# Graph attention over 100,000 edges: no memsets between the gathers, eight part gathers behind the last

## Chip, cores, metric

One core of a Trainium2 chip runs the kernel. The metric is the device time of one execution in microseconds; smaller is better.

## What is computed

6250 nodes with 96 features, 100,000 edges (src, dst) sorted by dst, and 96 features for each edge. With 8 heads of 12:

```python
Q, K, V = (x @ Wq + bq), (x @ Wk + bk), (x @ Wv + bv)       # per node
E = edge_attr @ We + be                                       # per edge
score = exp(clip(sum_head(K[src] * Q[dst] / sqrt(12) * E), -5, 5))
wV = segment_sum(V[src] * score, dst);  Z = segment_sum(score, dst)
out = layernorm(x + wV / (Z + 1e-6))
```

All in float32. The rows of K and V that the edges name in no order (`src`) have to be gathered; `dst` is sorted, so 512 edges in a row touch a window of fewer than 80 nodes.

## The kernel before

A first stage makes a table in device memory, `kv_table`, with a row of 192 values (K and V, 768 bytes) for each node, and `q_table` for Q. The edges are then worked off in 196 groups of 512 (`GROUPS`, `GROUP`), each of four tiles of 128 edges (the last group has two tiles, the very last tile 32 edges). All engines run the same sequence of groups, each at its own lag, held together by semaphores.

What each engine does for a group, in the variant `windowed(True)` that these inputs take:

- **GpSimd (POOL)** fetches the K and V rows of the four tiles with one indirect DMA each (`gather`, L490 to 495): one row of `kv_table` for each of 128 partitions, into one of 16 ring slots of `kv`. The first 8 groups (`EARLY`) gather rows of x instead, 32 gathers of 384 bytes a row, from which K and V are made on the core. Behind each gather stands a call of `space` (L497): a memset of 128 x 128 values of a buffer that nothing reads, with a wait for the memset before it.
- **TensorE** (L1015 to 1087) makes in its iteration i the product of the edge features of group i with We (L1023), the product that picks the query rows of group i (L1030), transposes the product of both of group i-2 (`turn`, L1041), and sums by node for group i-5 (`segment_sums`, L1055).
- **ScalarE** makes the one-hot matrix for the query product (L588, L591), copies the features' product out of PSUM (L597) and takes exponentials (L602, L603).
- **VectorE** (L870 to 896) multiplies queries and features of group i (L751), multiplies the gathered K rows of group i-2 with them (`times_keys`, L761; it waits for the group's four gathers and its turn), makes the one-hot matrix for the sums (L743), adds by head (L768), weighs the gathered V rows (L782) and adds a finished group's sums to the accumulator (L797).
- **SyncE (SP)** loads edge features, relative node numbers and query windows eight groups ahead (L414, L418, L422), and stores finished rows (L439).

Order of the gathers. Groups 8 to 15 go without a gate, 16 to 31 wait for the ring slot (`e_msg`: the group 16 before has been weighed). From group 32 on (`PACED_FROM`) each of the four gathers waits for a signal of TensorE, L518:

```python
pool.wait_ge(*((e_seg, group - 3), (e_e, ahead + 1), (e_q, ahead + 1), (e_turn, group + 1))[t])
```

with `ahead = group + 2`: the first for the sums of group-4, the second and third for the features' and the queries' product of group+2, the fourth for the turn of the group itself. In TensorE's order these are four steps in a row, from iteration group+1 to group+2.

Node rows that no later edge touches are divided, normalised and stored along the way; after the last group a short drain does the rest on VectorE and ScalarE, and SP stores it.

Of the kernel before, what the change touches and what calls it, by code (L numbers as in the profile page):

```python
# [31 lines left out]
F32 = mybir.dt.float32  # L32
# [7 lines left out]
P = 128  # L40
# [6 lines left out]
GROUP_TILES = 4  # L47
GROUP = GROUP_TILES * P
GROUPS = -(-N_EDGES // GROUP)
# [27 lines left out]
FIRST_TILES = [*range(0, NODE_TILES - LAST_TILES, FINAL_TILES), NODE_TILES - LAST_TILES, NODE_TILES]  # L77
STEPS = len(FIRST_TILES) - 1
FINAL_RING = 3
KV_RING, EA_RING, REL_RING, QWIN_RING, PICK_RING, MSG_RING = 16, 8, 8, 8, 4, 4  # L80
QE_RING = 3

# [12 lines left out]
def tiles_of(group):  # L95
    return min(GROUP_TILES, TILES - group * GROUP_TILES)


def edges_in(tile):
    return min(P, N_EDGES - tile * P)  # L100
# [25 lines left out]
def stores_of(step):  # L126

    first, n = FIRST_TILES[step], tiles_in(step)
    whole = min(n, N_NODES // P - first)
    return [(0, whole, P)] * (whole > 0) + [(whole, 1, N_NODES % P)] * (whole < n)  # L130


def stores_before(step):

    return sum(len(stores_of(s)) for s in range(step % FINAL_RING, step, FINAL_RING))


def build(nc, xT, x_rows, src_cols, dst_cols, dst_rows, eaT, weights, biases, ones, out):
# [16 lines left out]
    kv_table = nc.dram_tensor("kv_table", [TABLE_ROWS, 2 * DIM], F32).ap()  # L155
# [5 lines left out]
    with ExitStack() as ctx:  # L161
        def sb(name, shape, dt):
            return ctx.enter_context(nc.sbuf_tensor(name, shape, dt))
# [4 lines left out]
        def sem(name):  # L168
            return ctx.enter_context(nc.semaphore(name))
# [21 lines left out]
        stage_row = node_stage[:].rearrange("p t d -> p (t d)")  # L191
        result_cols, msg_cols = 2 * FINAL_RING * FINAL_TILES * DIM, MSG_RING * GROUP_TILES * SUMS
        results = stage_row[:, 0:result_cols].rearrange(
            "p (b s t d) -> p b s t d", b=2, s=FINAL_RING, t=FINAL_TILES)
        msg = stage_row[:, result_cols:][:, 0:msg_cols].rearrange(
# [6 lines left out]
        src_idx = sb("src_idx", [P, GROUPS * GROUP_TILES], U32)  # L202
# [21 lines left out]
        kv = sb("kv", [P, KV_RING, GROUP_TILES, 2 * DIM], F32)  # L224
# [11 lines left out]
        rows_f = acc_t[0:PAIRS, 0:2 * GROUP].rearrange("p (j e) -> p j e", j=2)  # L236


        spacer = sb("spacer", [P, 128], F32)
        g_src = sb("g_src", [P, GROUP_TILES], U32)  # L240
        g_dst = sb("g_dst", [P, GROUP_TILES], U32)
        g_dst_f = sb("g_dst_f", [P, GROUP_TILES], F32)
# [5 lines left out]

        z_inv = sb("z_inv", [P, FINAL_RING, FINAL_TILES, HEADS], F32)
        z_eps = sb("z_eps", [P, FINAL_RING, FINAL_TILES, HEADS], F32)  # L250
        stats = sb("stats", [P, FINAL_RING, FINAL_TILES, 6], F32)
        moments = sb("moments", [P, FINAL_RING, FINAL_TILES, 2], F32)
# [64 lines left out]
        e_msg = sem("e_msg")  # L317
        e_seg = sem("e_seg")
        e_acc = sem("e_acc")
        e_space = sem("e_space")  # L320
        g_free = sem("g_free")
        g_idx = sem("g_idx")
        g_step = sem("g_step")
# [31 lines left out]
        def path_of(eng):  # L355
            eng.wait_ge(r_ready, 1)
            return eng.value_load(path_i[0:1, 0:1], min_val=GENERAL, max_val=STREAMED)
# [6 lines left out]
        def all_tables_stored(eng):  # L364
            for i in range(UNITS_IN_RING):

                eng.wait_ge(d_table[i], 32 * len(range(i, UNITS, UNITS_IN_RING)))

        def by_path(eng, path, windowed, general):

            with eng.If(path == STREAMED):
                windowed(True)
            with eng.Else():
                with eng.If(path == WINDOWED):
                    windowed(False)
                with eng.Else():
                    general()
# [103 lines left out]
        @block.gpsimd  # L481
        def _(pool):
            nc.gpsimd.memset(ident[:], 0.0).then_inc(c_id0, 1)
            pool.wait_ge(c_id0, 1)
            nc.gpsimd.affine_select(out=ident[:], in_=ident[:], compare_op=ALU.not_equal, fill=1.0, base=0,
                                    pattern=[[-1, P]], channel_multiplier=1).then_inc(c_ident, 1)
            nc.gpsimd.iota(iota_i[:], pattern=[[1, SPAN]], base=0, channel_multiplier=0).then_inc(c_iota, 1)
            nc.gpsimd.iota(part_i[:], pattern=[[1, 1]], base=0, channel_multiplier=1).then_inc(c_iota, 1)

            def gather(rows, table, group, t, semaphore):  # L490
                tile = group * GROUP_TILES + t
                n = edges_in(tile)
                pool.indirect_dma_start(rows[0:n, :], None, table,  # L493
                                        bass.IndirectOffsetOnAxis(ap=src_idx[0:n, tile:tile + 1], axis=0)
                                        ).then_inc(semaphore, 16)

            def space(tile):  # L497
                if tile:
                    pool.wait_ge(e_space, tile)
                nc.gpsimd.memset(spacer[:], 0.0).then_inc(e_space, 1)  # L500

            pool.wait_ge(l_src_early, 16)
            for group in range(EARLY):
                for t in range(GROUP_TILES):
                    gather(kv[:, group, t, 0:DIM], x_rows, group, t, e_kv[group])
                    space(group * GROUP_TILES + t)
            pool.wait_ge(l_src, 16)
            all_tables_stored(pool)
            path = path_of(pool)

            def windowed(streamed):
                for group in range(EARLY, GROUPS):
                    slot, ahead = group % KV_RING, min(group + 2, GROUPS - 1)
                    if KV_RING <= group < PACED_FROM:
                        pool.wait_ge(e_msg, group - KV_RING + 1)
                    for t in range(tiles_of(group)):
                        if group >= PACED_FROM:
                            pool.wait_ge(*((e_seg, group - 3), (e_e, ahead + 1), (e_q, ahead + 1), (e_turn, group + 1))[t])  # L518
                        gather(kv[:, slot, t, :], kv_table, group, t, e_kv[slot])
                        space(group * GROUP_TILES + t)  # L520

            def general():
                pool.wait_ge(l_dst, 16)
                pool.wait_ge(x_kv, 2 * EARLY)
                with pool.Fori(0, GROUPS) as group:
                    pool.wait_ge(g_free, group + 1)
                    cols = bass.ds(group * GROUP_TILES, GROUP_TILES)
                    nc.gpsimd.tensor_copy(g_src[:], src_idx[:, cols]).then_inc(g_idx, 1)
                    nc.gpsimd.tensor_copy(g_dst[:], dst_idx[:, cols]).then_inc(g_idx, 1)
                    pool.wait_ge(g_idx, group * 2 + 2)  # L530
                    pool.sem_inc(g_step, 1)
                    for t in range(GROUP_TILES):
                        pool.indirect_dma_start(
                            kv[:, 0, t, :], None, kv_table,
                            bass.IndirectOffsetOnAxis(ap=g_src[:, t:t + 1], axis=0)).then_inc(g_gather, 16)
                        pool.indirect_dma_start(
                            g_q[:, t, :], None, q_table,
                            bass.IndirectOffsetOnAxis(ap=g_dst[:, t:t + 1], axis=0)).then_inc(g_gather, 16)

            by_path(pool, path, windowed, general)  # L540


# [605 lines left out]
```

## Time and profile before

| | |
|---|---|
| median of 3 timed runs | 1074.79 us (1072.62 to 1075.31) |
| span of the profiled execution, first to last instruction | 1231.7 us |
| busy in it: GpSimd, TensorE, VectorE, ScalarE | 919.8, 824.3, 595.7, 457.8 us |
| mean granted clock of TensorE | 0.81 of full speed |
| DMA: moved, mean rate | 153.29 MB, 124 GB/s |

The durations below come from the one profiled execution, whose own time is known by its span of 1231.7 us; the timed runs are executions without a profile. Busy time doesn't count semaphore waits or the issuing of plain DMAs. A gather is an instruction of POOL in the profile (DMA_INDIRECT), and its time is the time on POOL, not that until the data have landed. "remote" and "issue" in a row say that the idle time ahead of an instruction ended with an event that the profile can't name, or with none that it shows.

### The profile page before, as it was taken

The numbers are of one execution on the slowest core, as the hardware profiler recorded it, in microseconds if no ns is written. First come the engines' busy times: TensorE is split into PE (matmuls) and PEld (weight loads), VectorE is DVE, ScalarE is ACT, GpSimd is POOL, SyncE is SP. The second block draws the span as 40 slices with busy tenths as digits, with TensorE's granted clock in tenths as the row PEclk, the third lists the DMA queues.
The fourth block names the chain that finished last, engine by engine and source line by source line (L and its number), as shares of the span: only waits on it lengthen the run. The fifth ranks groups of instructions, "written<-read, shape, count | busy, mean of one in ns | idle before, by whom it ended". The sixth has DMA issues, their size and how long they took to land.

```text
span 1231.7 us, 13818 instructions
## 1 busy us (share of the span) xinstructions
PE 824.3 (67%) x3375; PEld 455.9 (37%) x3375; DVE 595.7 (48%) x1583; ACT 457.8 (37%) x1094; POOL 919.8 (75%) x1572
## 2 busy tenths in 40 slices
PE   6518565986676666667676667666767676776763
PEld 4415232543343333333333334333333333333433
DVE  5104344954444464445444545445554545454645
ACT  3206232743343343333333334333434343433331
POOL 8882777167878778778787787887777877877783
PEclk9757787988877888887888787887878877878885
DMA  9922344454545445445444444444444444444321
GB/s 245 277 77 77 104 126 109 137 145 120 144 116 138 125 112 131 125 111 127 122 121 125 108 135 117 120 132 120 111 130 125 128 127 112 121 130 126 92 77 51
DMA packets 124525, 153.29 MB, mean 124 GB/s; under 512 B 57885, under 2 KB 92191, under 8 KB 124436
## 3 DMA queue, kind: packets, MB, share of 16 engines
q0 software_dynamic: 37008, 75.28, 23.9%
q1 hardware_dynamic: 80608, 73.74, 21.7%
q10 hardware_dynamic: 6822, 3.31, 1.0%
q8 instruction: 31, 0.51, 0.2%
q14 instruction: 56, 0.46, 0.1%
HBM read 142.26 MB, written 9.98 MB: 124 GB/s over the span
## 4 chain that ended last, share of the span: by engine, by line
POOL 37%; PE 22%; issue 16%; another core or an unknown queue 10%; DVE 6%; DMA 6%; ACT 2%; SPq 0%; DVEq 0%; POOLq 0%
POOL kv L493 30%; POOL spacer L500 7%; DMA kv<-kv_table,src_idx 5%; PE ps_eq L1030 4%; PE ps_eq L1023 4%; PE ps_qe_seg L1055 3%; PE ps_last L1055 3%; PE ps_eq_qe L1023 2%; PE ps_qe_seg L1041 2%; PE ps_eq_qe L1030 1%; PE ps_eq_qe L1041 1%; DVE ps_last L768 1%; DVE node_stage L743 1%; DMA w_all<-biases_in 1%
## 5 line engine op out<-in xcount | busy, mean ns | idle before, releaser
L493 POOL DMA_INDIRECT kv<-kv_table,src_idx x750 | 714.2, 952 | 285.5 <-issue 114.7
L602 ACT ACTIVATE ps_last<-clipped 128x32 f32<-128x32 f32 x196 | 39.4, 201 | 542.4 <-issue 397.2
L1030 PE MATMUL ps_eq<-pick_t,q_win 128*96 128x512 f32 (+1 forms) x262 | 169.5, 735 | 78.7 <-ACT e_t L597 58.4
L761 DVE TENSOR_TENSOR kq<-kv,ps_qe_seg 128x384 f32<-128x384 f32 x98 | 53.9, 550 | 260.7 <-DMA kv<-kv_table,src_idx 195.7
L1023 PE MATMUL ps_eq<-ea,w_all 128*96 128x512 f32 (+1 forms) x262 | 172.5, 747 | 8.1 <-issue 7.4
L500 POOL MEMSET spacer<- 128x128 f32 x782 | 172.8, 221 | 2.7 <-remote 2.2
L761 DVE TENSOR_TENSOR kq<-kv,ps_eq_qe 128x384 f32<-128x384 f32 x98 | 54.1, 552 | 238.3 <-DMA kv<-kv_table,src_idx 175.5
L1055 PE MATMUL ps_qe_seg<-node_stage 128*104 128x80 f32 x784 | 116.2, 306 | 54.5 <-issue 28.9
L1055 PE MATMUL ps_last<-node_stage 128*104 128x80 f32 x780 | 108.2, 292 | 49.3 <-issue 24.2
L588 ACT ACTIVATE distance<-rel_bc,neg_part 80x512 bf16<-80x512 bf16 x196 | 138.4, 706 | 1.8 <-issue 0.6
L1055 PEld LDWEIGHTS ps_qe_seg<-node_stage 128*104 128x104 f32 x784 | 105.2, 218 | 64.6 <-issue 49.6
L591 ACT ACTIVATE pick_t<-distance 80x512 f32<-80x512 bf16 x196 | 123.2, 629 | 6.2
L1055 PEld LDWEIGHTS ps_last<-node_stage 128*104 128x104 f32 x780 | 97.7, 205 | 58.0 <-issue 33.5
L1030 PEld LDWEIGHTS ps_eq<-pick_t,q_win 128*96 128x96 f32 x262 | 46.4, 199 | 195.0 <-issue 194.4
L597 ACT COPY e_t<-ps_eq 96x512 f32<-96x512 f32 x131 | 74.3, 567 | 92.6 <-remote 58.2
L768 DVE TENSOR_REDUCE ps_last<-kq 128x32 f32<-128x384 f32 x196 | 107.6, 549 | 0.1
L782 DVE TENSOR_TENSOR node_stage<-kv,ps_last 128x384 f32<-128x384 f32 x196 | 106.3, 542 | 0.0
L1041 PE MATMUL ps_qe_seg<-ident,qe_t 96*128 96x96 f32 x390 | 60.0, 285 | 65.9 <-issue 41.2
L1030 PE MATMUL ps_eq_qe<-pick_t,q_win 128*96 128x512 f32 x130 | 82.6, 722 | 31.7 <-issue 15.8
L1041 PEld LDWEIGHTS ps_qe_seg<-ident,qe_t 96*128 96x128 f32 x390 | 48.3, 164 | 146.1 <-issue 103.4
L751 DVE TENSOR_TENSOR qe_t<-e_t,ps_eq 96x512 f32<-96x512 f32 x131 | 88.3, 674 | 17.5 <-PE ps_eq L1030 8.9
L1041 PEld LDWEIGHTS ps_eq_qe<-ident,qe_t 96*128 96x128 f32 x392 | 48.3, 160 | 125.9 <-issue 92.3
(90 smaller groups left out, 788.2 us busy)
## 6 DMA issues: line engine op xcount, KB each, us to landing
ea<-ea_t_in SPq DMA_DIRECT2D x196, 192.0 KB
rel_bc<-rel_rows_dram SPq DMA_DIRECT2D x196, 80.0 KB
kv<-kv_table,src_idx POOLq DMA_INDIRECT x750
q_win<-q_table SPq DMA_DIRECT2D x196, 30.0 KB
kv_table<-node_stage SPq DMA_DIRECT2D x5, 576.0 KB
x_both<-x_t_in SPq DMA_DIRECT2D x5, 480.0 KB, 8.9
x_both<-x_rows_in ACTq DMA_DIRECT2D x10, 240.0 KB
out<-node_stage SPq DMA_DIRECT2D x11, 192.0 KB
```

The lines of the kernel that those rows point to most:

```text
L493: pool.indirect_dma_start(rows[0:n, :], None, table, bass.IndirectOffsetOnAxis(ap=src_idx[0:n, tile:tile + 1], axis=0)).then_inc(semaphore ...
L500: nc.gpsimd.memset(spacer[:], 0.0).then_inc(e_space, 1)
L588: nc.scalar.activation(distance[:, b, 0:n], rel_bc[:, slot, 0:n], ACT.Abs, bias=neg_part[0:WINDOW, :]).then_inc(e_dist, 1)
L591: nc.scalar.activation(pick_t[0:WINDOW, group % 3, 0:n], distance[:, b, 0:n], ACT.Relu, bias=1.0, scale=-1.0).then_inc(e_pt, 1)
L751: nc.vector.tensor_tensor(qe_t[:, group % QE_RING, 0:n], e_t[:, group % 2, 0:n], ps_eq[(2 * group + 1) % 3][0:DIM, 0:n], ALU.mult).then_in ...
L761: nc.vector.tensor_tensor(kq[:, group % 2, 0:n, :], kv[:, slot, 0:n, 0:DIM], ps_qe[group % 2][:, 0:n * DIM].rearrange("p (t d) -> p t d", ...
L768: nc.vector.tensor_reduce(score[:, group % 2, 0:n, :], kq[:, group % 2, 0:n, :].rearrange("p t (h d) -> p t h d", h=HEADS), axis=AX_X, op= ...
L782: nc.vector.tensor_tensor(m[:, :, 0:DIM].rearrange("p t (h d) -> p t h d", h=HEADS), kv[:, group % KV_RING, 0:n, DIM:2 * DIM].rearrange("p ...
L1023: nc.tensor.matmul(ps_eq[2 * group % 3][0:DIM, 0:n], w_e, ea[:, slot, 0:n], start=True, stop=True).then_inc(e_e, 1)
L1030: nc.tensor.matmul(ps_eq[(2 * group + 1) % 3][0:DIM, 0:n], q_win[:, slot, :], pick_t[:, group % 3, 0:n], start=True, stop=True).then_inc(e ...
L1041: last = nc.tensor.transpose(ps_qe[group % 2][:, t * DIM:(t + 1) * DIM], qe_t[:, group % QE_RING, t * P:(t + 1) * P], ident[0:DIM, 0:DIM])
L1055: last = nc.tensor.matmul(ps_seg[group % 2][0:SUMS, 0:WINDOW], msg[:, group % MSG_RING, t, :], pick[:, group % PICK_RING, t, :], start=(t ...
```

## The change

The buffer `spacer`, its semaphore and the function `space` go, so that gathers follow each other on POOL with nothing but their own waits between them. The waits at L515 and L518 stay. Behind the last gather of group 195 POOL waits until group 180 has been weighed, issues eight more gathers of 127, 125, 121, 120, 112, 64, 16 and 2 rows of `kv_table` into slots 4 and 5 of the ring, which nothing reads any more, and waits for them.

```diff
+PARTS = (127, 125, 121, 120, 112, 64, 16, 2)
...
-        spacer = sb("spacer", [P, 128], F32)
...
-        e_space = sem("e_space")
+        e_part = sem("e_part")
...
-            def space(tile):
-                if tile:
-                    pool.wait_ge(e_space, tile)
-                nc.gpsimd.memset(spacer[:], 0.0).then_inc(e_space, 1)
-
             pool.wait_ge(l_src_early, 16)
             for group in range(EARLY):
                 for t in range(GROUP_TILES):
                     gather(kv[:, group, t, 0:DIM], x_rows, group, t, e_kv[group])
-                    space(group * GROUP_TILES + t)
...
                         gather(kv[:, slot, t, :], kv_table, group, t, e_kv[slot])
-                        space(group * GROUP_TILES + t)
+                part_gathers()
+
+            def part_gathers():
+
+                slot = GROUPS % KV_RING
+                pool.wait_ge(e_msg, GROUPS - KV_RING + 1)
+                for i, n in enumerate(PARTS):
+                    pool.indirect_dma_start(kv[0:n, slot + i // GROUP_TILES, i % GROUP_TILES, :], None, kv_table,
+                                            bass.IndirectOffsetOnAxis(ap=src_idx[0:n, i:i + 1], axis=0)
+                                            ).then_inc(e_part, 16)
+                pool.wait_ge(e_part, 16 * len(PARTS))
```

## Rows read from the trace of the kernel before

**Rows 1.** The page: span, and busy time of each engine with its share and instructions

```profile
span 1231.7 us, 13818 instructions
...
PE 824.3 (67%) x3375; PEld 455.9 (37%) x3375; DVE 595.7 (48%) x1583; ACT 457.8 (37%) x1094; POOL 919.8 (75%) x1572
```

**Rows 2.** The page: the chain that ended last, by line, shares of the span

```profile
POOL kv L493 30%; POOL spacer L500 7%; DMA kv<-kv_table,src_idx 5%; PE ps_eq L1030 4%; PE ps_eq L1023 4%; PE ps_qe_seg L1055 3%; PE ps_last L1055 3%; PE ps_eq_qe L1023 2%; PE ps_qe_seg L1041 2%; PE ps_eq_qe L1030 1%; PE ps_eq_qe L1041 1%; DVE ps_last L768 1%; DVE node_stage L743 1%; DMA w_all<-biases_in 1%
```

**Rows 3.** The page's groups of instructions: busy us, mean ns, idle before

```profile
L493 POOL DMA_INDIRECT kv<-kv_table,src_idx x750 | 714.2, 952 | 285.5 <-issue 114.7
...
L500 POOL MEMSET spacer<- 128x128 f32 x782 | 172.8, 221 | 2.7 <-remote 2.2
```

**Rows 4.** Instructions of L493, the first 32 gathers: ns min/median/max, first and last start

```profile
L493 POOL DMA_INDIRECT kv<-x_rows_in,src_idx x32: 950/950/2569, 4.6 to 49.0; - x32
```

**Rows 5.** The waits of all engines: us in total, times, longest

```profile
DVE kq L761 <- DMA kv<-kv_table,src_idx: 371.2, 131, 5.4
```

**Rows 6.** POOL's timeline: start us, us, what

```profile
255.28 0.95 POOL L493 DMA_INDIRECT kv<-kv_table,src_idx  x1 [0.17 <-issue]
256.23 0.22 POOL L500 MEMSET spacer<- 128x128 f32 x1
256.62 0.95 POOL L493 DMA_INDIRECT kv<-kv_table,src_idx  x1 [0.17 <-issue]
```

**Rows 7.** L761 by stretches: its busy time (x instructions), clock, DMA share, GB/s

```profile
119.00:219.00 100.00, 9.03 (x17) 0.78 0.43 118
219.00:254.00 35.00, 7.35 (x14) 1.00 0.49 133
254.00:1215.00 961.00, 90.25 (x163) 0.81 0.46 121
```

**Rows 8.** L493 in the paced stretch, the same columns

```profile
254.00:1215.00 961.00, 621.88 (x653) 0.81 0.46 121
```

**Rows 9.** All engines while POOL pauses: busy us of PE, PEld, DVE, ACT, POOL

```profile
219.00:254.00 35.00, 33.50 (x193) 20.34 (x193) 34.93 (x93) 27.26 (x65) 0.06 (x1) 1.00 0.49 133
```

**Rows 10.** POOL's timeline, group 32's first gather

```profile
253.94 0.95 POOL L493 DMA_INDIRECT kv<-kv_table,src_idx  x1 [34.98 <-PE ps_qe_seg L1055]
```

**Rows 11.** POOL's timeline, two gathers behind a stop

```profile
460.00 0.95 POOL L493 DMA_INDIRECT kv<-kv_table,src_idx  x1 [1.92 <-remote]
...
477.71 0.95 POOL L493 DMA_INDIRECT kv<-kv_table,src_idx  x1 [1.84 <-remote]
```

**Rows 12.** Timeline of all engines, 278 to 288 us

```profile
278.89 0.49 PE L1041 MATMUL ps_qe_seg<-ident,qe_t 96*128 96x96 f32 x4
...
283.41 0.56 DVE L761 TENSOR_TENSOR kq<-kv,ps_eq_qe 128x384 f32<-128x384 f32 x1 [2.53 <-DMA kv<-kv_table,src_idx]
...
284.75 0.55 DVE L782 TENSOR_TENSOR node_stage<-kv,ps_last 128x384 f32<-128x384 f32 x1
...
287.75 0.58 ACT L597 COPY e_t<-ps_eq_qe 96x512 f32<-96x512 f32 x1 [0.46 <-PE ps_eq L1023]
...
287.85 0.95 POOL L493 DMA_INDIRECT kv<-kv_table,src_idx  x1 [1.77 <-remote]
```

**Rows 13.** Timeline of all engines in the unpaced stretch, 193 to 206 us

```profile
193.86 1.94 PE L1023 MATMUL ps_eq<-ea,w_all 128*96 128x512 f32 x2
...
202.01 0.95 POOL L493 DMA_INDIRECT kv<-kv_table,src_idx  x1 [0.17 <-issue]
...
205.09 0.58 ACT L597 COPY e_t<-ps_eq 96x512 f32<-96x512 f32 x1 [13.64 <-remote]
```

**Rows 14.** Timeline of the end

```profile
1215.28 0.88 POOL L493 DMA_INDIRECT kv<-kv_table,src_idx  x1 [0.17 <-issue]
...
1217.01 9.79 SPq L439 DMA_DIRECT2D out<-node_stage  x4
1217.58 0.35 DVE L761 TENSOR_TENSOR kq<-kv,ps_qe_seg 128x192 f32<-128x192 f32 x1 [0.97 <-DMA kv<-kv_table,src_idx]
```

**Rows 15.** DMA queues of the page: packets, MB, share of 16 engines

```profile
q0 software_dynamic: 37008, 75.28, 23.9%
```

## Prediction

> **What bounds the kernel now.** I read the page's head, its chain and its groups first. GpSimd (POOL) is busy for 919.8 of 1231.7 us, TensorE for 824.3 and VectorE for 595.7 [rows 1]; the chain that ended last gives 30% to the gathers of L493 and 7% to the spacers of L500 [rows 2]. The groups are 782 gathers of 0.95 us and 782 memsets of 0.22 us [rows 3, 4], and the waits show VectorE's product with the gathered keys (L761) idle for 371.2 us until gathers land [rows 5]. Then POOL's timeline: the memset starts where the gather ends, the next gather 0.17 us behind the memset, and gathers start 1.34 us apart [rows 6]. Four make 5.34 us for a group of 512 edges.
>
> Is that the group's period? Between 254 and 1215 us VectorE makes 163 groups' products in 961 us, 5.90 us each, over 653 gathers, 1.472 us each [rows 7, 8]. So 1.336 of 1.472 us is POOL's own step and 0.136 us (89 us in all) is waiting. What the others could do shows where POOL pauses: from 219 to 254 us they live on sixteen groups gathered ahead and do 14 in 35 us, 2.5 us each, with TensorE at clock 1.00 (2.4 GHz) and busy for 33.50 us, 2.4 us a group [rows 7, 9]. They need less than half of the period; POOL sets it.
>
> The 89 us come as holds: POOL stops some 1.6 us about every 17.7 us, as before 460.00 and 477.71 [rows 11]. One from near by: the gather at 287.85 is the fourth of group 37 (counted from 253.94 [rows 10], group 32's first), and its gate, the turn of group 37, is by the same counting the one of 278.89, done 8.5 us before. ScalarE's copy, which waits for a TensorE signal too, starts at 287.75 [rows 12]. Signals of TensorE seem to reach the others late while gathers run, and at once when POOL stops. The unpaced stretch shows it stronger: a product over the features ends at 195.80, and ScalarE takes it at 205.09 after 13.64 us of idling, 2 us after the last gather of a run ended at 202.96 [rows 13].
>
> **Profile and timed runs.** The span is 1231.7 us, the median 1074.79: the profiled execution is 157 us longer. POOL's instructions alone give 782 x 1.336 = 1045 us, with 4.6 us before the first gather and 15.5 us from the end of the last to the end 1065 us [rows 4, 6, 14], 10 us under the median. If the steps last as long there, timed runs hardly wait and are POOL's chain from end to end; the holds and most of the slow start would belong to the profiled execution. I subtract POOL's saving from both, and keep the holds for the rivals.
>
> **The change, part by part.**
>
> *Spacers go.* 782 memsets of 0.22 us [rows 3], and with each a wait for the memset before, long satisfied. What then stands between two gathers, no row shows. Bounds: the gap of 0.17 us goes too, a step is 0.95 us and 0.386 us are saved; or it stays, the step is 1.12 us and 0.216 us are saved [rows 6]. A gain below 0.216 would need longer gathers, a loss gathers over 1.34 us; the nearest row for that is the longest of the first 32, 2.57 us, once, beside the loads of the start [rows 4]. I take the gap to stay: every gather has it ahead, no memset has. In the paced stretch that is 653 x 0.216 = 141 us (bound 252). The first 128 gathers could give 28 us (bound 49), but the others need 34 iterations of 2.5 us before group 32's gather may go, and in the profile they come so late that POOL idles for 34.98 us [rows 10]. I count half, 14 us.
>
> The Trainium skill, GPSIMD Engine Reference, section "Instruction dispatch", warns that a core of GpSimd starts the next instruction as soon as it has done its own share of the last. By that rule the gap needn't stand between two gathers, and the sum would be that of the first rival below. The memsets, which follow gathers without a gap, agree with it; the 0.17 us ahead of every gather does not.
>
> *The gates stay.* From group 32 on each gather waits for a TensorE signal, and a faster POOL meets them closer. The round: a fourth gather lands 1.4 us after its end (1216.16 to 1217.58) [rows 14], product to weighing take 1.9 us (283.41 to 285.30) [rows 12], TensorE's sums, features, queries and turn 2.4 us, the gather 1.12 us: 7 us. The turn of group g follows the sums of g-4, weighed behind the keys of g-3, so that is for three groups, 2.3 us each: no bound. With a signal 8.5 us late it is 15.5 us, 5.2 us each, and would bind; that is for the rivals. At TensorE's lower level (1.2 GHz) its 2.4 us become 4.8, over POOL's 4 x 1.12 = 4.48. The mean clock of 0.81 puts 38% of the stretch at that level [rows 7]: 0.3 us x 0.38 x 163 = 19 us at most; I take 10 us back, since less idling should keep the clock up more often.
>
> *DMA.* Gathers come up to 19% faster; the queues' share in the stretch goes from 0.46 [rows 7] to 0.55 at most. Nothing.
>
> *Eight gathers at the end.* Issued from 1216.2 on: 8 x 1.12 = 9 us, landing 1.4 us later, POOL is done near 1226.7. VectorE's drain and the last stores (four issued between 1217.01 and 1226.80, the end at 1231.7) [rows 14] hide it with 5 us to spare; without that cover it would cost all of 10 us. Their gate is satisfied long before, and 687 rows of 768 bytes are 0.53 MB. Bounds: 0 and 10 us; I take 0.
>
> The Trainium skill, DMA: Bandwidth & Descriptors, section "Why a DMA increments its semaphore by 16 and not by 1", has a DMA use the largest number of engines, up to 16, that divides its partitions: one for 127, five for 125, eleven for 121, fifteen for 120. No row shows such a gather. The queue's row, 23.9% of sixteen engines for 75.28 MB [rows 15], gives 63 us of one engine per MB, so an estimate by this rule is 6 us on one engine for 127 rows; if the last stores queued behind it the sum would be 6 us more, 936.
>
> **Sum.** 1074.8 - 141 - 14 + 10 = 930 us. For the profiled span 1231.7 - 141 + 10 = 1101, since POOL doesn't set the start there.
>
> **The rivals.**
>
> *The gap goes too.* Step 0.95 us: 1074.8 - 252 - 14 = 809, and with all of the start 774, less what the lower clock takes (a group of 3.8 us against 4.8): about 800. For it: memsets need no gap. 0.12.
>
> *Holds take part of it.* POOL meets late signals sooner: 0.6 holds of 1.6 us per group against 0.33 now, 4.48 + 0.96 = 5.44 against 5.90 us, 75 us saved: 1000 us. For it: the late signals of [rows 12]. Against: a gate not met stops POOL, and the stop lets all signals through. 0.15.
>
> *Slower: gathers without a spacer hold TensorE's signals up.* Place: POOL's gates in the paced stretch. If the 0.39 us between gathers is what lets signals pass, each group needs a stop: 4.48 + 1.6 = 6.08 us against 5.90, 163 x 0.18 = 30 us, 1105; if timed runs had no holds before, 0.74 x 163 = 120 us, 1195. It decides from 0.89 holds per group. For it: the unpaced stretch, 17 groups in 100 us although their keys lay ready [rows 7], and the 13.64 us [rows 13]. Against: a median that leaves 10 us for all holds. 0.21.
>
> *No change.* The round with late signals sets the period (5.2 us above, with landings of 2 us 5.4), and what POOL saves becomes waiting at its gates: 1072 to 1078. Against: 1.336 us steps fill the median already. 0.05.
>
> **How the numbers follow.** The forecast has 0.47 (its own range 890 to 960), the others as above. About 0.3% is what a measurement of this kernel can tell from no change: faster by more 0.74, within 0.05, slower 0.21. The range goes from 800, the bound without a gap, to 1105, the slower case at its nearer price; its farther half and a little below 800 are left out.
>
> **What would show it.** No memsets of L500; gathers starting 1.12 us apart (0.95 for the first rival); about 4.6 us per group between group 32 and the end, plus holds; L761's idle time before landings down from 371 us by some 140; no more than 0.4 holds per group; eight more gathers behind the last, none in the chain. Wrong if gathers lengthen back to back (over 1.3 us each nothing is left), if stops of 1.6 us come in nearly every group, or if POOL's end takes the place of the last stores.

## The result, and the profile after

The changed kernel takes 1014.51 us (1013.26 to 1015.47, 4 runs) where the kernel before takes 1074.63 us (1072.62 to 1075.31, 4 runs): a ratio of 0.9444, with a 95% interval of 0.943 to 0.9457, so 60 us faster. The forecast was 930 us and 145 us faster. The direction was right, the size was not. In every run here the timed figure is 1.8 to 2.0 us longer than the span of the same execution (1014.0 against 1012.2).

The page of the changed kernel, head, a queue's row, chain by line and the gathers' group, against [rows 1, 15, 2, 3]:

```profile
span 1012.2 us, 13044 instructions
...
PE 757.0 (75%) x3375; PEld 417.5 (41%) x3375; DVE 594.2 (59%) x1583; ACT 452.7 (45%) x1094; POOL 751.9 (74%) x798
...
q0 software_dynamic: 37712, 75.81, 28.7%
...
POOL kv L493 35%; DMA kv<-kv_table,src_idx 16%; PE ps_eq L1034 3%; PE ps_eq L1027 3%; PE ps_last L1059 2%; DVE node_stage L747 2%; DVE ps_last L772 2%; PE ps_eq_qe L1027 2%; PE ps_eq_qe L1034 2%; PE ps_qe_seg L1059 1%; DVE kq L765 1%; PE ps_qe_seg L1045 1%; PE ps_eq_qe L1045 1%; DMA q_table<-node_stage 1%; POOL kv L521 1%
...
L493 POOL DMA_INDIRECT kv<-kv_table,src_idx x750 | 709.6, 946 | 233.8 <-issue 196.6
```

The 172.8 us of memsets are gone, the gathers last as long as before (946 against 952 ns), and the chain is still that of the gathers and of their landings. But their idle time ahead, 233.8 us for 750, is 0.31 us each. GpSimd's timeline shows it, against [rows 6]:

```profile
399.23 0.95 POOL L493 DMA_INDIRECT kv<-kv_table,src_idx  x1 [0.30 <-issue]
...
400.49 0.95 POOL L493 DMA_INDIRECT kv<-kv_table,src_idx  x1 [0.31 <-PE ps_eq_qe L1045]
...
401.74 0.95 POOL L493 DMA_INDIRECT kv<-kv_table,src_idx  x1 [0.30 <-issue]
```

Gathers start 1.25 us apart, not 1.12: between two gathers stand 0.30 us, where 0.17 stood between a memset and a gather. The second row names TensorE as what ended the 0.31 us, but the gap is the same where nothing was waited for; a releaser beside a gap of the plain size is no hold.

The longest waits, against [rows 5], and the time of L765 (VectorE's product with the keys, L761 before) by stretches, against [rows 7]:

```profile
DVE kq L765 <- DMA kv<-kv_table,src_idx: 361.7, 162, 5.1
POOL kv L493 <- issue: 205.7, 658, 5.5
```

```profile
119.00:219.00 100.00, 11.33 (x21) 0.90 0.60 161
219.00:254.00 35.00, 4.18 (x8) 0.95 0.57 155
254.00:988.00 734.00, 80.78 (x146) 0.86 0.52 140
```

VectorE still waits 361.7 us for landings. No stop of 1.6 us as in [rows 11] is left, and no pause of 35 us as in [rows 10]: from 254 us on a group takes 734/146 = 5.03 us, and 4 x 1.25 is 5.00. Behind 254 us no gap ahead of a gather is over 0.5 us: the gates (the waits of L518) hold no gather here.

The end, against [rows 14]: GpSimd's and VectorE's last instructions.

```profile
988.57 0.88 POOL L493 DMA_INDIRECT kv<-kv_table,src_idx  x1 [0.30 <-issue]
989.75 2.55 POOL L521 DMA_INDIRECT kv<-kv_table,src_idx  x1 [0.30 <-issue]
992.60 1.20 POOL L521 DMA_INDIRECT kv<-kv_table,src_idx  x1 [0.30 <-issue]
994.11 1.02 POOL L521 DMA_INDIRECT kv<-kv_table,src_idx  x1 [0.30 <-issue]
995.43 0.97 POOL L521 DMA_INDIRECT kv<-kv_table,src_idx  x1 [0.30 <-issue]
996.71 0.96 POOL L521 DMA_INDIRECT kv<-kv_table,src_idx  x1 [0.31 <-issue]
997.97 0.91 POOL L521 DMA_INDIRECT kv<-kv_table,src_idx  x1 [0.30 <-issue]
999.18 0.86 POOL L521 DMA_INDIRECT kv<-kv_table,src_idx  x1 [0.30 <-issue]
...
999.64 0.81 DVE L862 TENSOR_SCALAR node_stage<-node_stage,moments,rstd 128x96 f32<-128x96 f32 x3 [0.67 <-ACT rstd L617]
1000.35 0.88 POOL L521 DMA_INDIRECT kv<-kv_table,src_idx  x1 [0.30 <-issue]
```

The eight part gathers (called the eight below; 127, 125, 121, 120, 112, 64, 16 and 2 rows, in that order) take 11.8 us with their gaps, the first alone 2.55. GpSimd is done at 1001.23, behind VectorE's last instruction (1000.45), and the span ends 11.8 us behind VectorE, where before it ended 5.7 us behind it (1225.98 to 1231.7). What is still moving in the last 7.7 us of the changed kernel, by the DMA queues between 1004.5 and 1012.2 us:

```profile
q14 instruction: 4, 0.03, 1.3%
```

That is the only queue with packets there: the gathered rows and the stored ones have landed by then.

### The profile page after: what moved, and what is told of

The parts are those of the page before. It is cut to its first block, busy times and chain, and to the rows that moved or that the text cites. A ratio compares the mean times of both kernels' runs of the same rounds, so it can differ in the third digit from the quotient of the medians.

```text
span 1012.2 us, 13044 instructions
## 1 busy us (share of the span) xinstructions
PE 757.0 (75%) x3375; PEld 417.5 (41%) x3375; DVE 594.2 (59%) x1583; ACT 452.7 (45%) x1094; POOL 751.9 (74%) x798
## 4 chain that ended last, share of the span: by engine, by line
POOL 36%; PE 19%; DMA 18%; issue 15%; DVE 7%; ACT 3%; SPq 0%; DVEq 0%; ACTq 0%
POOL kv L493 35%; DMA kv<-kv_table,src_idx 16%; PE ps_eq L1034 3%; PE ps_eq L1027 3%; PE ps_last L1059 2%; DVE node_stage L747 2%; DVE ps_last L772 2%; PE ps_eq_qe L1027 2%; PE ps_eq_qe L1034 2%; PE ps_qe_seg L1059 1%; DVE kq L765 1%; PE ps_qe_seg L1045 1%; PE ps_eq_qe L1045 1%; DMA q_table<-node_stage 1%; POOL kv L521 1%
## 5 line engine op out<-in xcount | busy, mean ns | idle before, releaser
L493 POOL DMA_INDIRECT kv<-kv_table,src_idx x750 | 709.6, 946 | 233.8 <-issue 196.6
L1034 PE MATMUL ps_eq<-pick_t,q_win 128*96 128x512 f32 (+1 forms) x262 | 161.3, 702 | 19.5 <-ACT e_t L601 18.2
L1027 PE MATMUL ps_eq<-ea,w_all 128*96 128x512 f32 (+1 forms) x262 | 158.9, 692 | 7.3 <-DVE qe_t L755 5.8
L765 DVE TENSOR_TENSOR kq<-kv,ps_qe_seg 128x384 f32<-128x384 f32 x98 | 54.0, 551 | 187.8 <-DMA kv<-kv_table,src_idx 187.7
L765 DVE TENSOR_TENSOR kq<-kv,ps_eq_qe 128x384 f32<-128x384 f32 x98 | 54.1, 552 | 174.0 <-DMA kv<-kv_table,src_idx 174.0
L1059 PE MATMUL ps_qe_seg<-node_stage 128*104 128x80 f32 x784 | 101.7, 280 | 57.0 <-DVE acc_t L801 43.4
L1059 PE MATMUL ps_last<-node_stage 128*104 128x80 f32 x780 | 102.9, 282 | 54.9 <-DVE acc_t L801 45.9
L1059 PEld LDWEIGHTS ps_qe_seg<-node_stage 128*104 128x104 f32 x784 | 91.5, 193 | 65.4 <-DVE node_stage L786 50.4
L1059 PEld LDWEIGHTS ps_last<-node_stage 128*104 128x104 f32 x780 | 92.1, 195 | 63.9 <-DVE node_stage L786 53.8
L747 DVE TENSOR_TENSOR node_stage<-ps_last,rel_f 128x320 f32<-128x320 f32 x196 | 94.5, 482 | 0.5 <-ACT ps_last L606 0.5
L1027 PE MATMUL ps_eq_qe<-ea,w_all 128*96 128x512 f32 x130 | 84.4, 737 | 4.4 <-DVE qe_t L755 4.4
L1045 PE MATMUL ps_qe_seg<-ident,qe_t 96*128 96x96 f32 x390 | 54.7, 266 | 36.6 <-DVE kq L765 36.5
L1034 PE MATMUL ps_eq_qe<-pick_t,q_win 128*96 128x512 f32 x130 | 75.4, 665 | 6.3 <-ACT e_t L601 5.9
```

The source lines that it names most:

```text
L493: pool.indirect_dma_start(rows[0:n, :], None, table, bass.IndirectOffsetOnAxis(ap=src_idx[0:n, tile:tile + 1], axis=0)).then_inc(semaphore ...
L747: nc.vector.tensor_tensor(pick[:, group % PICK_RING, 0:n, :], window_iota.unsqueeze(1).to_broadcast([P, n, WINDOW]), rel.unsqueeze(2).to_b ...
L765: nc.vector.tensor_tensor(kq[:, group % 2, 0:n, :], kv[:, slot, 0:n, 0:DIM], ps_qe[group % 2][:, 0:n * DIM].rearrange("p (t d) -> p t d", ...
L1027: nc.tensor.matmul(ps_eq[2 * group % 3][0:DIM, 0:n], w_e, ea[:, slot, 0:n], start=True, stop=True).then_inc(e_e, 1)
L1034: nc.tensor.matmul(ps_eq[(2 * group + 1) % 3][0:DIM, 0:n], q_win[:, slot, :], pick_t[:, group % 3, 0:n], start=True, stop=True).then_inc(e ...
L1045: last = nc.tensor.transpose(ps_qe[group % 2][:, t * DIM:(t + 1) * DIM], qe_t[:, group % QE_RING, t * P:(t + 1) * P], ident[0:DIM, 0:DIM])
```

## The experiments

Chips are of two sorts for this kernel: on some the kernel before has a median of 1071 to 1075 us (the first sort below), on others of 1218 to 1232 us (the second), and no single run of it lay between (1070 to 1075 and 1214 to 1239 us). No chip was measured at two times, so whether this belongs to the chip or to a state that it was in isn't shown. Each kernel ran beside the kernel before on the same chip, and kernels with the same number in the second column shared a chip; across chips only ratios are compared. The result above is of the first sort; the trace that the prediction was read from, 1231.7 us long, looks like the second. Of the kernel before there is no trace on the first sort.

| kernel | before there, us | median, us | ratio, 95% interval |
|---|---|---|---|
| changed kernel, again | 1071.02 | 1012.17 | 0.9448 (0.9433 to 0.9464) |
| changed kernel, a third time | 1071.37 | 1012.97 | 0.9449 (0.9433 to 0.9464) |
| without the eight | 1073.66 | 1008.98 | 0.9399 (0.9384 to 0.9415) |
| without the eight and the gates, 1 | 1071.02 | 1006.70 | 0.9396 (0.938 to 0.9412) |
| without the eight and the gates, 2 | 1073.66 | 1008.84 | 0.9398 (0.9383 to 0.9414) |
| without the eight and the gates, 3 | 1071.37 | 1006.23 | 0.939 (0.9374 to 0.9406) |
| without the eight and the gates, with one-column spacer | 1073.66 | 1008.93 | 0.9395 (0.938 to 0.9411) |
| before, 256-column spacer | 1073.66 | 1157.70 | 1.0782 (1.0764 to 1.08) |
| without the eight | 1217.77 | 1230.17 | 1.0103 (1.0078 to 1.0128) |
| without the eight | 1231.42 | 1240.94 | 1.0084 (1.006 to 1.0108) |
| before, one-column spacer | 1217.77 | 1232.32 | 1.0134 (1.0104 to 1.0164) |
| before, one-column spacer | 1231.42 | 1247.31 | 1.014 (1.0111 to 1.0169) |
| before, one-column spacer with semaphore | 1217.77 | 1232.37 | 1.0127 (1.0103 to 1.0152) |
| before, with the eight | 1217.77 | 1220.12 | 1.0035 (1.0014 to 1.0056) |
| before, with the eight | 1231.42 | 1236.95 | 1.0054 (1.0029 to 1.008) |
| changed, other sizes of the eight | 1231.42 | 1250.53 | 1.0168 (1.0138 to 1.0197) |
| changed, other sizes of the eight | 1231.61 | 1252.49 | 1.016 (1.0101 to 1.0218) |
| without the eight and the gates, 4 | 1231.61 | 1337.93 | 1.0854 (1.0792 to 1.0916) |

**Is GpSimd's step (from the start of one gather to the start of the next) all that bounds?** The spacer made larger, in the kernel before:

```
-        spacer = sb("spacer", [P, 128], F32)
+        spacer = sb("spacer", [P, 256], F32)
```

> The kernel before with a spacer of 256 columns in place of 128. Theory A (GpSimd's step is the whole bound): each of the 782 steps longer by the memset's growth, which from 0.22 us for 128 columns is 0.05 to 0.13 us; 40 to 100 us slower than the kernel before where that takes 1071 us. Theory C (something else bounds too): less than half of the growth. Where the kernel before takes 1220 to 1230 us: GpSimd has idle time, so less than half of the growth is seen.

Its timeline on GpSimd, start and duration:

```profile
399.32 0.95 POOL L493 DMA_INDIRECT kv<-kv_table,src_idx  x1 [0.16 <-issue]
400.26 0.34 POOL L500 MEMSET spacer<- 128x256 f32 x1
400.76 0.95 POOL L493 DMA_INDIRECT kv<-kv_table,src_idx  x1 [0.16 <-issue]
```

A step of 1.45 us against the 1.34 of [rows 6]: 782 x 0.11 = 86 us, and 84.0 us were measured. That is theory A: on this sort of chip the time is 782 of GpSimd's steps and a start and an end around them, and a change to the step comes through whole.

**What is the gap of 0.30 us?** A memset of one column, without semaphore, in place of the spacer:

```
             def space(tile):
-                if tile:
-                    pool.wait_ge(e_space, tile)
-                nc.gpsimd.memset(spacer[:], 0.0).then_inc(e_space, 1)
+                nc.gpsimd.memset(spacer[:, tile:tile + 1], 0.0)
```

It ran three times: twice in the kernel before with its gates, and once added to the kernel without gates and without the eight.

> No waits on signals, no eight gathers, and a memset of one column after each gather. Where the kernel before takes 1071 us: Theory A (0.30 us is the gap between two DMA instructions, 0.17 us the one after a memset) a step of 1.22 us and 985 us, from 975 to 1000, with 1006.7 us without the memset; Theory B (0.30 us follows a gather in any case) 1071 us or more. Where the kernel before takes 1220 to 1230 us: near the kernel without waits and memset.

Its timeline on GpSimd:

```profile
399.95 0.95 POOL L494 DMA_INDIRECT kv<-kv_table,src_idx  x1 [0.19 <-issue]
400.90 0.11 POOL L499 MEMSET spacer<- 128x1 f32 x1
401.20 0.95 POOL L494 DMA_INDIRECT kv<-kv_table,src_idx  x1 [0.19 <-issue]
402.15 0.11 POOL L499 MEMSET spacer<- 128x1 f32 x1
```

Both theories miss: it takes 1008.93 us, and the kernel without it on the same chip 1008.84. The memset lies inside the 0.30 us: 0.95 + 0.11 + 0.19 is again 1.25. With 128 columns the sum is 0.95 + 0.22 + 0.17 = 1.34, with 256 it is 0.95 + 0.33 + 0.17 = 1.45 (0.34 and 0.16 in the rows shown). So some 0.30 us pass behind a gather before the next one, whether it is empty or a short memset fills it, and a memset adds only what it has beyond about 0.13 us. The step of 1.12 us that the forecast took was not to be had by taking the spacer out.

> The kernel before, with a spacer of one column in place of 128 and no semaphore on it. Theory A (the gap of 0.30 us is that between two DMA instructions on the queue of GpSimd, and one after a memset is 0.17): a step of 0.95 + memset of some 0.1 + 0.17 = 1.22 us, against 1.25 without a spacer; with the end as before about 985 us, from 975 to 1010. Theory B (0.30 us follows a gather whatever comes next, so a memset is only added to it): a step of 1.35 or more, 1075 us or above. Theory C (TensorE's signals start to hold the gathers up once the step is under some 1.25): no better than 1007 us, with idle time ahead of gathers put down to TensorE.

> As the spacer of one column, but with the semaphore set by it and waited for by the next. If the semaphore costs nothing on GpSimd: the same time as with no semaphore, within 3 us. If the signalling is a part of the spacer's price (a spacer took 0.22 us and the gap behind it 0.17): 0.02 to 0.06 us a step more, 15 to 50 us above the kernel without it.

> A spacer of one column and no semaphore, again, for a ground where the kernel before takes 1071 us. Theory A (0.30 us is the gap between two DMA instructions of GpSimd, 0.17 the one after a memset): a step of 0.95 + some 0.1 + 0.17 = 1.22 us; with the end as before about 985 us, from 975 to 1010. Theory B (0.30 us follows a gather whatever comes next): a step of 1.35 or more, 1071 us or above. Theory C (signals of TensorE hold gathers up once the step is under 1.25 us): no better than 1007 us. If the kernel before takes 1218 us again: 1232 us as in the first run.

These three fell on the second sort of chip, where nothing is to be gained by a shorter step (below): 1.0134, 1.0127 with the semaphore, and 1.014. The semaphore makes no difference within the intervals. The expected 975 to 1010 us can't be tested by the time there, but the step can: unhindered gathers start 1.25 us apart in all three traces, with a memset of 0.11 us and a gap of 0.19 us, where theory A had 1.22 and theory B 1.35.

**Do the gates hold gathers?** Without them (and without the eight) only the wait for a free slot stays:

```
-                    if KV_RING <= group < PACED_FROM:
+                    if KV_RING <= group:
                         pool.wait_ge(e_msg, group - KV_RING + 1)
                     for t in range(tiles_of(group)):
-                        if group >= PACED_FROM:
-                            pool.wait_ge(*((e_seg, group - 3), (e_e, ahead + 1), (e_q, ahead + 1), (e_turn, group + 1))[t])
...
-                part_gathers()
```

> The changed kernel without the eight gathers, and without the waits of the gathers on TensorE's and VectorE's signals; only the wait for a free slot stays, once a group. Where the kernel before takes 1075 us: no difference from a step of 1.25 us if the waits never hold a gather (1007 us within 3); if packed gathers delay others, slower. Where it takes 1218 us: Theory S1 (each signal that a gather waits for arrives late, and the waits are what makes it long): under 1100 us. Theory S2 (the gathers' own activity makes the signals late, and TensorE's chain is the bound): 1230 us or more.

> As before, the changed kernel without the waits on signals and without the eight gathers. Where the kernel before takes 1071 us: 1006.7 us again. Where it takes 1220 to 1230 us: Theory S1 (the gathers' waits on late signals make it long) under 1100 us; Theory S2 (TensorE's chain is the bound whatever GpSimd does) 1230 us or more.

> The changed kernel without the waits on signals and without the eight gathers, for the chips where the kernel before takes 1218 to 1231 us. Theory S1 (there the late signals hold the gathers, and the waits are what makes it long): the gathers run through at 1.25 us, under 1100 us. Theory S2 (TensorE's signals to VectorE and ScalarE are late too, and that chain is the bound): 1230 us or more, with the gathers held by the free slots. Where the kernel before takes 1071 to 1075 us: 0.94 of it, as twice.

0.9396, 0.9398 and 0.939 against 0.9399 with the gates; on the one chip that had both, 1008.84 against 1008.98 us. On the first sort of chip they cost and give nothing. The last of the three was meant for the second sort and fell on the first.

**What do the eight cost?**

```
                         gather(kv[:, slot, t, :], kv_table, group, t, e_kv[slot])
-                part_gathers()
```

> The changed kernel without the eight gathers, once more. Where the kernel before takes 1071 us: Theory A (the eight set the end) 1006 us, as without the waits (1006.7 us); Theory B (hidden) 1012 us. Where it takes 1220 to 1230 us: 1% slower than the kernel before, as twice.

> The changed kernel as it is, since the first four runs stood on a ground where the kernel before took 1217.8 us and not 1074.6. Where the kernel before takes 1075 us: 1014.5 us again. Where it takes 1218 us (TensorE's signals late, gathers held by their waits): Theory S (the late signals set that time, spacers or not): 1230 to 1240 us, no faster than before.

The changed kernel's ratio was 0.9448 and 0.9449; without the eight it is 0.9399: 0.005 of 1071 us, 5.3 us. The theory that the eight set the end holds; its 1006 us were for a chip at 1071 us, and this one was at 1073.66. Two chips had both the changed kernel and the one without the eight and the gates: there it is 5.5 us (1012.17 against 1006.70) and 6.7 us (1012.97 against 1006.23). The last instructions of the kernel without them, on GpSimd and VectorE:

```profile
989.55 0.88 POOL L493 DMA_INDIRECT kv<-kv_table,src_idx  x1 [0.30 <-issue]
...
1000.57 0.81 DVE L861 TENSOR_SCALAR node_stage<-node_stage,moments,rstd 128x96 f32<-128x96 f32 x3 [0.67 <-ACT rstd L616]
```

VectorE ends 10.95 us behind the last regular gather, as with the eight (11.00), and the span (1007.4) 6.0 us behind VectorE. With the eight it ends 11.0 us behind the last of them (1001.23 to 1012.2). So VectorE isn't slowed on this sort; the end waits for GpSimd's tail and for what comes behind it. Of the 11.0 us behind the last gather the landing of data is at most 3.3 (up to 1004.5 us, above); what the other 7.7 are isn't shown, nor whether the gathers or GpSimd's wait for them bring them in, since no run has the one without the other. This version, 1008.98 us, beats both kernels on the first sort.

Other sizes, 112 rows in place of the first four, were to tell whether the sizes or the number cost:

```
-PARTS = (127, 125, 121, 120, 112, 64, 16, 2)
+PARTS = (112, 112, 112, 112, 112, 64, 16, 2)
```

> The changed kernel with other sizes of the last eight gathers: 112 rows five times, 64, 16 and 2, in place of 127, 125, 121, 120, 112, 64, 16 and 2. Theory P1 (the end waits for as many instructions as there are, 1.2 us each; the one of 127 rows adds 1.6): 2 us under the changed kernel, 1010 us. Theory P2 (only gathers of odd sizes land late and hold the end): 6 to 7 us under, 1006 us. Theory P3 (hidden): 1012 us, the same.

> The changed kernel with 112 rows five times, 64, 16 and 2 as its last eight gathers. Where the kernel before takes 1071 to 1075 us: Theory P1 (the eight cost by the time that they take on GpSimd, behind which the end waits; the one of 127 rows takes 2.55 us and 112 rows 0.96): 2 us under the changed kernel, 0.943 of the kernel before. Theory P2 (only the odd sizes cost): 0.939 to 0.940, as without the eight. Theory P3 (sizes do not matter): 0.9448. Where it takes 1218 to 1231 us: 1.017 times, as in the first run.

It ran twice, both times on the second sort of chip, where its end is another one (VectorE 10.7 us behind GpSimd, 1245.11 against 1234.42 in the second run). Its timeline there, the last regular gather, the first and the last of the eight, and VectorE:

```profile
1223.80 0.88 POOL L493 DMA_INDIRECT kv<-kv_table,src_idx  x1 [0.31 <-issue]
1224.99 0.94 POOL L521 DMA_INDIRECT kv<-kv_table,src_idx  x1 [0.30 <-issue]
...
1233.54 0.88 POOL L521 DMA_INDIRECT kv<-kv_table,src_idx  x1 [0.30 <-issue]
1234.89 0.24 DVE L801 TENSOR_TENSOR acc_t<-acc_t,ps_qe_seg 104x80 f32 x1 [7.72 <-remote]
```

So 2.55 us is the price of 127 rows and not of the first place; 112 rows take 0.94 there. What each of the eight costs in time to the end on the first sort stays open. The last row shows what the eight do on the second sort: VectorE stands for 7.72 us while they run. TensorE's sums for it end at 1227.82; the trace's record of semaphores has their signal at 1234.77, 0.35 us behind the end of the last gather. VectorE ends 20.4 us behind the last regular gather there, and 10.9 in the kernel without the eight. The eight added to the kernel before:

> The kernel before with its spacers, and the eight gathers added after the last one. Theory A (they lie on the end): 7 us slower than the kernel before, about 1082 us. Theory B (hidden behind the weighing and the stores of the last group): 1075 us within 2.

> The kernel before with its spacers and the eight gathers added. Theory A (the eight set the end, by as much as in the changed kernel): 7 us slower than the kernel before, 1078 us. Theory B (hidden): 1071 us. If the kernel before takes 1218 us again: 1220 us as in the first run.

1.0035 and 1.0054 of the kernel before, 4 and 7 us by the ratios (2.4 and 5.5 by the medians), both intervals above 1: the eight aren't hidden there either, but theory A's 7 us are not settled by this. In the first of the two the span ends 22.50 us behind the last regular gather, in the kernel before 15.54.

**The other sort of chip.** The kernel without the eight is 1% slower than the kernel before there, where on the first sort it is 6% faster.

> The changed kernel without the eight gathers at the end. Theory A (the eight set the end: from the end of the last regular gather to the end of the span it is 22.8 us in the changed kernel and 15.5 us before): about 7 us less than the 1014.5 us of the changed kernel, so 1007 us. Theory B (the last stores set the end anyway, as the prediction had it): 1014 us within 2.

> The changed kernel without the eight gathers, again, for a ground where the kernel before takes 1071 us. Theory A (the eight set the end): 7 us under the changed kernel, 1005 to 1007 us, and the same as without the waits on signals (1006.7 us). Theory B (hidden): 1012 us. If the kernel before takes 1218 us again: 1230 us as in the first run.

Neither theory on the eight had 1230 or 1241 us; they were for the first sort. The second run was expected to be 1% slower here again, and is 0.8%. Waits of the second of these runs:

```profile
DVE kq L764 <- DMA kv<-kv_table,src_idx: 386.4, 129, 5.7
POOL kv L493 <- issue: 233.9, 673, 24.1
POOL kv L493 <- remote: 84.0, 53, 2.8
ACT e_t L600 <- remote: 81.4, 36, 16.3
```

and its group of gathers:

```profile
L493 POOL DMA_INDIRECT kv<-kv_table,src_idx x750 | 709.6, 946 | 465.6 <-issue 224.4 <-remote 84.0 <-PE ps_qe_seg L1058 49.2
```

Unhindered gathers are 1.25 us apart there too. Idle time beyond the gaps is 465.6 - 750 x 0.30 = 241 us, and was 285.5 - 750 x 0.17 = 158 us with the spacers [rows 3]: 83 us more of waiting. The steps save 750 x (0.22 - 0.13) = 68 us and the gathers 5; the sum is +10 us, and 9.5 were measured (the two profiled spans, from different chips, differ by 6.1). What the spacers' going saves comes back, and a little more, as stops at the gates. Then the gates were taken away there:

> The changed kernel without the waits on signals and without the eight gathers, tried again for a chip where the kernel before takes 1218 to 1231 us. Theory S1 (the gathers' waits on late signals make it long): under 1100 us. Theory S2 (TensorE's late signals to VectorE and ScalarE make it long): 1230 us or more. Where the kernel before takes 1071 to 1075 us: 0.939 of it again.

```profile
ACT e_t L598 <- remote: 523.1, 67, 16.1
...
POOL kv L493 <- DVE node_stage L783: 274.2, 53, 20.5
```

It is 106 us slower than the kernel before (1.0854), theory S2. ScalarE now waits 523.1 us, up to 16.1 us at a time, for signals whose sender had ended long before. One of them, from the timeline of all engines of that run (counted from the start, both rows are of group 80; ScalarE copies a product while TensorE is at the next):

```profile
604.33 1.04 PE L1024 MATMUL ps_eq<-ea,w_all 128*96 128x512 f32 x2
...
612.78 0.94 POOL L493 DMA_INDIRECT kv<-kv_table,src_idx  x1 [0.30 <-issue]
613.94 0.58 ACT L598 COPY e_t<-ps_eq 96x512 f32<-96x512 f32 x1 [6.87 <-remote]
```

The product over the features ends at 605.37 by its modelled end, and ScalarE takes it 8.6 us later, after 6.87 us of idling; in between GpSimd gathers every 1.25 us. In the changed kernel on the first sort of chip the same pair of group 80 reads:

```profile
397.93 1.04 PE L1027 MATMUL ps_eq<-ea,w_all 128*96 128x512 f32 x2
...
401.64 0.56 ACT L601 COPY e_t<-ps_eq 96x512 f32<-96x512 f32 x1
```

Here ScalarE comes 2.7 us behind the product and idles for none of it. The trace's record of semaphores tells the two apart: the product's signal is there at 398.99, 0.01 us behind the product's end, and on the second sort at 613.91, 8.5 us behind the end and 0.03 us ahead of the copy. The product itself takes 1.04 us in both, so this isn't TensorE's clock. Over all 196 groups, a product's signal is recorded more than 0.5 us late with ScalarE's copy within 0.1 us behind it in none in the changed kernel on the first sort; on the second in 64 groups of the trace of before (median 5.5 us late), in 72 without the eight (4.1), and in 87 without the gates too (11.0).

So on the second sort TensorE's signals do come late. That the running gathers hold them up rests on when they come: without the gates 49 of the 87 late ones arrived while GpSimd stood still for over 0.5 us, which it did for 310 of 1335 us, and at the end of the kernel with other sizes one came as the last gather ended. Gathers came every 1.25 or 1.34 us in all runs on that sort, so this cause is likely and not shown. By it a gate that stops GpSimd lets signals through, and without gates each group waits longer for TensorE than the stops cost. The changed kernel with its eight did not run on that sort; its nearest kin there are 0.8 to 1.0% slower than the kernel before without the eight, and 1.6 to 1.7% with eight of other sizes.

> The changed kernel itself, for the same chips. From its version without the eight gathers, 1.01 and 1.008 times the kernel before there, and the eight, 1.0035 and 1.005: 1.013 to 1.016 times, about 1240 us. Where the kernel before takes 1071 to 1075 us: 0.944 to 0.945 of it again.

That run fell on the first sort and repeated the result.

## Why the prediction was right and wrong

**GpSimd sets the time: right.** 84 of 86 us of a longer spacer come through, and the saving is 782 steps' worth. That the timed runs of before hardly wait (1065 us of steps, start and end against a median of 1074.8) fits the chips that they ran on: in the longer spacer's trace GpSimd's gaps exceed the plain one by more than 0.2 us only six times, by 3.6 us in all.

**The saving per step: the step that failed.** "I take the gap to stay", at 0.17 us, made a step of 1.12 us and terms of 141 and 14 us. The gap between two gathers is 0.30 us. The prediction said that no row shows what stands between two gathers, and bounded it by 0 and 0.17 us; for a smaller gain it thought of longer gathers, not of a longer gap. At 1.25 us the paced stretch gives 653 x 0.086 = 56 us and the first gathers 128 x 0.086 = 11 us, all of it, since nothing else bounds the start here. That is 67 us where 155 stood. The rival without any gap fell with it. VectorE's wait for landings was to drop by some 140 us; it is 361.7 us against 371.2, in traces of the two sorts.

The Trainium skill, GPSIMD Engine Reference, "Instruction dispatch", whose rule was weighed for that rival, has a core start the next instruction as soon as it has done its share; memsets behind gathers do, but between two gathers 0.30 us stand, and no run here shows less.

**The eight gathers: costed at nothing, cost 5.3 us.** Three parts were off. They take 11.8 us and not 9 (2.55 us for 127 rows, and gaps of 0.30); VectorE ends 11.0 us behind the last regular gather, so GpSimd passes it by 0.8 us; and what lies behind GpSimd's last gather is 11.0 us, where the sum had 1.4 us for the landing and an end 5 us later, and where 6 lie behind VectorE's last instruction. The stated upper bound of 10 us holds, and "if POOL's end takes the place of the last stores" is what happened. The Trainium skill, DMA: Bandwidth & Descriptors, "Why a DMA increments its semaphore by 16 and not by 1", from which 6 us were estimated for 127 rows, agrees in its order with the durations on GpSimd, 2.55, 1.20, 1.02, 0.97 and 0.96 us for one, five, eleven, fifteen and sixteen engines; that the 5.3 us are those of the 127 rows isn't shown.

**The clock: 10 us were taken back, none was due.** The mean clock of the span is 0.868, 0.86 behind 254 us. The 0.81 of before [rows 7] is of the second sort; on the first the kernel before had 0.842 to 0.867 in the runs beside others, and the changed one 0.865 to 0.890. TensorE isn't the bound: all of the step's saving comes through.

**The sum, mended.** 1074.6 - 67 + 5 = 1013 us, and 1014.5 were measured.

**Signals of TensorE.** The 8.5 us that were read from [rows 12] hold: by count the turn of group 37 ends at 279.38, and its gather starts at 287.85. The reading of [rows 13] pairs two groups: the product that ends at 195.80 is group 18's, and the copy at 205.09 is group 17's, whose product ended at 184.90, 20.2 us before. The signals were later than the prediction had it.

**The rivals.** "Holds take part", 1000 us, came nearest in number and was wrong in mechanism: there isn't one hold. The slower rival, that gathers without a spacer hold TensorE's signals up, goes the way of the other sort of chip, which is slower by 0.8 to 1.0%; its prices of 1105 to 1195 us were for the timed runs, and no run shows them.

**The profiled execution.** The prediction put the 157 us between trace and median down to the profiled execution. The timed runs of the kernel before that take 1218 to 1232 us agree with the trace's 1231.7, so the 157 us fit the chip and not the profiling; the forecast span of 1101 us has its kin there at 1228.6 and 1237.8 us. Which property of a chip makes TensorE's signals late stays open: no kernel here told that.

## What to carry to other kernels

Taking a filler out between two instructions saves its duration and the gap beside it (0.22 + 0.17 us here) less the gap that the bare pair has (0.30): look for a place in the trace where the pair already stands bare, and without one bound the new gap from above by the whole of the old distance. Where the profiled execution is 15% longer than the median, treat it as another machine: read the mechanism from it, and try the change on both before it is called good for all. Pair a wait with the instruction that it waits for by counting both from the start; engines that run one group apart make neighbours in time look like a pair. What a tail of small gathers costs isn't told by their landing: here 11.0 us lay behind the last of them and 6 us behind VectorE's last instruction, so by these two numbers it would have had to end some 5 us ahead of VectorE to be hidden (an estimate).

## What the runs showed of the hardware

- Behind an indirect gather of 128 rows (0.95 us) GpSimd starts the next 0.30 us later; a memset of 0.11 us fits inside that gap for nothing (1.25 us a step with and without it), one of 0.22 us makes the step 1.34, one of 0.33 us 1.45.
- An indirect gather takes GpSimd 2.55 us for 127 rows, 1.20 for 125, 1.02 for 121, 0.97 for 120, 0.96 for 112, 0.91 for 64, 0.86 for 16 and 0.88 for 2: fewer rows save almost nothing, 127 cost 1.6 us more than 128.
- The same kernel takes 1071 to 1075 us on some chips and 1218 to 1232 on others. On the others TensorE's signals are recorded late (more than 0.5 us late with ScalarE waiting in 57 to 87 of 196 groups in the eleven traces there, by a median of 4.1 to 11.0 us; in at most one group in the nine traces of the first); ScalarE waited up to 16.3 us at a time; and waits that stop GpSimd were worth 7.5 to 7.7% there (1.0854 against 1.0103 and 1.0084) and nothing on the first.
- The changed kernel's span ends 11.0 us behind GpSimd's last gather; in the last 7.7 of them only the instruction queue moves data.
